# Masked down product over pairs of ring places, with its loads and its search reordered

## The chip, the cores and the metric

One Trainium2 chip, one core. The metric is the device time of one execution in microseconds; lower is better.

## The reference

Four residual sublayers over 2,048 tokens (two sequences of 1,024) of width 512: causal attention with 32 heads of 16, an FFN with 4-bit quantised weights (inner width 1,792), a masked MLP (inner width 1,376), and the same FFN again. The change lies in the masked MLP:

```python
s = silu(x @ w_gate.T)                      # x: layernormed, 1376 wide
_, idx = top_k(-abs(s), 688)                # the 688 smallest of each row
s = s with zeros at idx
y = (s * (x @ w_up.T)) @ w_down.T           # back to 512 wide
```

## The kernel before

`phase_project` and `phase_attend` run first (until about 670 us) and are not touched. `phase_mlp` (L1190) does the FFN, the masked MLP and the second FFN.

**Chunks and stages.** The tokens are eight chunks (`NC = 8`) of 256, each of two tiles of 128 (`TPC = 2`, t = 0, 1). A chunk k goes through four stages: f1 k (FFN), gates k, down k, f2 k (FFN). `mlp_order` (L1822) interleaves the stages of several chunks: f1 0, gates 0, f1 1, f1 2, gates 1, **down 0**, f1 3, gates 2, f2 0, **down 1**, f1 4, gates 3, f2 1, **down 2**, f1 5, gates 4, **down 3**, f2 2, gates 5, f1 6, **down 4**, f2 3, gates 6, f1 7, **down 5**, f2 4, gates 7, **down 6**, f2 5, f2 6, **down 7**, f2 7. So down 0, 3 and 6 follow their own gates stage at once; before the others there is at least one FFN stage in between.

**Slots.** A stage is a row of slots, one unit of TensorE work each: 14 in an FFN stage (`block_of`, L1497, and two slots behind it `product`, L1511), 8 in gates (`gate_unit`, L1521: four column blocks, each for both tiles), 8 in down (`product_tk`, L1539). What every other engine does is written into the slots by `mlp_stages` (L1837), and each engine walks the slots in the same order. Operands are split into fp16 high and low halves, so that each product is three matmuls.

**The masked path.** After gates k, VectorE and ScalarE search each row's threshold in 31 trials (`search`, L1646; `signs`, L1580), then VectorE finishes the masks in 18 items (`finish`, L1662): 7 for tile 0, 11 for tile 1. Behind a tile's last item come `mask` on GpSimd (L1459, two halves), `masked_high` on ScalarE (L1613), `masked_low` on GpSimd (L1465), and the **turn** (`turn_masked`, L1413): one DMA transpose of the tile from ax to pp, issued by SyncE three slots after the first mask. Down k multiplies the turned tiles by w_down.

**Where the search is paced.** L1907 to L1922 spread the items over the slots: `costs` are the items' times, `spans` those of a slot on TensorE (3860 ns in an FFN stage, 3460 in gates, 1950 in down), and the rate is set so that all of a chunk's items are done before the last slots ahead of its down stage, which the end of L1911 leaves out.

**The ring.** Four places (`ring`, L1215) hold either gate and up weights (`load_g`, L1390: eight loads f = 0 to 7 of a gates stage, 688 KB each, place f % 4) or the down weights (`load_d`, L1401: d = 0 to 3, place d; d = 3 is shorter and comes in two DMAs). In down, `product_tk` goes through d = 0 to 3 with tile 0 and then with tile 1, 9, 9, 9 and 6 matmuls each; d = 0 first waits for the tile's turn (`mt_in`), and each d with tile 0 for its place. Places come free as tile 1 is done with them: loads of the next gates stage wait for `DG + f + 1` units. In a gates stage, loads f = 4, 5 stand in slot 1, f = 6, 7 in slot 3 (they wait for 4 units), d = 0, 1 in slot 5 (6 units) and d = 2, 3 in slot 7 (8 units).

**The shifts.** The normed input of a coming stage is transposed by two DMA transposes (`Norm.shift`, L1310), one a tile, from d_xs to xT. In a gates stage both stand in slot 5, for the stage after it (or the one after the down stage, where down comes next).

**SyncE's queue.** SyncE issues all of these in the order of its program: in each slot first the shifts, then the turns, then the loads, then stores and refills (L1429 to L1442). A wait there holds back all that is behind it.

```python
for u, t in slot.shifts:
    norms[u.name].shift(sp, u, t)
for k, t in slot.masked_turns:
    turn_masked(k, t)
for k, f in slot.gate_loads:
    load_g(k, f)
for k, d in slot.down_loads:
    load_d(k, d)
```

Of the kernel before, what the change touches and what calls it, by code (L numbers as in the profile page):

```python
# [1189 lines left out]
def phase_mlp(nc, ident, w_gate, w_up, w_down, wgu_scr, wd_scr, x1_scr, out):  # L1190

    TPC = 2
# [6 lines left out]
    DG = -(-TKB // DB)  # L1199
    DU = TPC * DG  # L1200
    RING = 4
    XR = 5
# [6 lines left out]
    with ExitStack() as ctx:  # L1209
# [173 lines left out]
        def _(sp):  # L1383
# [6 lines left out]
            def load_g(k, f):  # L1390
                c, m, r = f // 2, f % 2, f % RING
                if f >= RING:
                    wait(sp, gm_ok, GU * k + TPC * (c - 1))
                elif k == 1:
                    wait(sp, gm_ok, TPC * ((f + RING) // 2 + 1))
                elif k > 1:
                    wait(sp, dm_ok, DU * (k - 2) + DG + f + 1)
                sp.dma_start(ring[r][:, 0:2 * KB * TKW], wgu_scr[m, c].rearrange("p a k w -> p (a k w)")
                             ).then_inc(ring_in[r], 16)

            def load_d(k, d):  # L1401
                if k + 1 < NC:
                    wait(sp, gm_ok, GU * (k + 1) + TPC * (3 + d // 2))
                else:
                    wait(sp, dm_ok, DU * (k - 1) + DG + d + 1)
                full = min(DB, TKB - 1 - DB * d)
                sp.dma_start(ring[d][:, 0:full * 2 * D].rearrange("p (j w) -> p j w", j=full),
                             wd_scr[DB * d:DB * d + full].rearrange("j p a d -> p j (a d)")).then_inc(ring_in[d], 16)
                if full < DB:
                    sp.dma_start(ring[d][0:ROWS_LAST, full * 2 * D:(full + 1) * 2 * D],  # L1410
                                 wd_scr[TKB - 1, 0:ROWS_LAST].rearrange("p a d -> p (a d)")).then_inc(ring_in[d], 16)
# [17 lines left out]
            for s in stages:  # L1429
                for slot in s.slots:  # L1430
                    for u, t in slot.shifts:
                        norms[u.name].shift(sp, u, t)
                    for k, t in slot.masked_turns:
                        turn_masked(k, t)
                    for k, f in slot.gate_loads:
                        load_g(k, f)
                    for k, d in slot.down_loads:
                        load_d(k, d)
                    for done in slot.stores:
                        store(done)  # L1440
                    for c in slot.refills:
                        load_x(c)  # L1442
# [53 lines left out]
        def _(pe):  # L1496
# [42 lines left out]
            def product_tk(s, v):  # L1539
                k, t, d = s.c, v // DG, v % DG  # L1540
                if d == 0:
# [98 lines left out]
        def _(dve):  # L1640
# [79 lines left out]
            def take_in(s, t):  # L1720

                if s.kind == "down":
                    dve.wait_ge(dm_ok, DU * s.c + DG * (t + 1))
                else:
                    dve.wait_ge(dn_ok, JB * (s.f + 1))
# [94 lines left out]


def mlp_order(NC):  # L1822

# [13 lines left out]
def mlp_stages(NC, GU, DU, TPC, RING, DG, XR):  # L1837
# [70 lines left out]
    for n, (p, slot, span, duty) in enumerate(own):  # L1908
        rate = 0
        for k in range(NC):  # L1910
            ahead = [(l, d) for q, _slot, l, d in own[n:] if q < at["down", k]][:-2]  # L1911
            left = sum(costs[item] for c, item in items if c <= k)
# [10 lines left out]
    assert not items  # L1923

    everywhere = [slot for s in stages for slot in s.slots]
    for n, slot in enumerate(everywhere):
# [9 lines left out]
    for k in range(NC):  # L1936
        for f in range(2 * TKC):
# [4 lines left out]
            elif k > 1:  # L1942
                stages[at["down", k - 2]].slots[DG + f].gate_loads.append((k, f))
        for d in range(DG):
            if k + 1 < NC:
                stages[at["gates", k + 1]].slots[TPC * (3 + d // 2) - 1].down_loads.append((k, d))
            else:
                stages[at["down", k - 1]].slots[DG + d].down_loads.append((k, d))
    for p, s in enumerate(stages[:-1]):
# [35 lines left out]
```

## Time and profile before

| | |
|---|---|
| median of 3 runs | 1968.83 us (1966.81 to 1973.61) |
| the profiled execution | 1973.73 us, its span 1971.9 us |
| TensorE busy, matmul | 1837.5 us, 93% of the span |
| VectorE busy | 1430.5 us, 73% |
| ScalarE busy | 1031.7 us, 52% |
| GpSimd busy | 762.1 us, 39% |
| mean granted TensorE clock | 0.977 of full speed |
| DMA q1 (issued by SyncE) | 187.77 MB, 33.5% of 16 engines' span |

The busy share is of the whole span, phases with other limits included; `ring<-wd_scr` is a load of down weights, `ring<-wgu_scr` one of gate or up weights, `pp<-ax` a turn and `xT_f<-d_xs` a shift. `acc<-ring,pp` is the masked down product, `ga<-ring,xT_g` and `ub<-ring,xT_g` are the two halves of a gate unit.

### The profile page before, as it was taken

How to read it: one execution, taken by the hardware profiler on the slowest of the kernel's cores; microseconds unless marked ns; L12 is line 12 of the kernel's file. 1: busy time of each engine (PE TensorE's matmuls, PEld its weight loads, DVE VectorE, ACT ScalarE, POOL GpSimd, SP SyncE). 2: the span in 40 equal slices, each digit the busy share in tenths (PEclk: the TensorE clock that was granted, in tenths of full speed). 3: DMA queues.
4: the chain of work that ended last, by engine and by line, in shares of the span. 5: the costliest groups of instructions: out<-in, count | busy, mean ns of one | idle time of the engine just before them, and what ended most of it. 6: DMA issues, size and time to landing. Idle time of an engine off the chain costs nothing.

```text
span 1971.9 us, 39587 instructions
## 1 busy us (share of the span) xinstructions
PE 1837.5 (93%) x14968; PEld 1123.6 (57%) x14968; DVE 1430.5 (73%) x2798; ACT 1031.7 (52%) x1888; POOL 762.1 (39%) x922
## 2 busy tenths in 40 slices
PE   7998888898899798999999999999999999989979
PEld 3443333333333475775776776666776766747746
DVE  6567778788882313987888988887888789869821
ACT  4234677777785122654654645535546546536411
POOL 4685756566762111223215124132151151322331
PEclk9998899999999898999999999999999999999989
DMA  7864544555434604106131331225142142071010
GB/s 236 236 198 141 151 118 122 139 149 159 147 112 125 218 1 126 12 12 176 49 126 42 90 125 42 90 75 144 57 122 73 40 133 73 12 201 34 12 40 12
DMA packets 217133, 205.70 MB, mean 104 GB/s; under 512 B 136400, under 2 KB 173264, under 8 KB 216992
## 3 DMA queue, kind: packets, MB, share of 16 engines
q1 hardware_dynamic: 210992, 187.77, 33.5%
q0 software_dynamic: 4272, 12.91, 2.0%
q10 hardware_dynamic: 1728, 3.15, 0.4%
q8 instruction: 87, 1.43, 0.3%
q14 instruction: 54, 0.44, 0.1%
HBM read 147.39 MB, written 33.62 MB: 92 GB/s over the span
## 4 chain that ended last, share of the span: by engine, by line
PE 53%; DVE 5%; POOL 3%; issue 2%; DMA 2%; ACT 1%; SPq 0%; DVEq 0%; ACTq 0%
PE acc L1517 13%; PE ga L1507 13%; PE ub L1507 13%; PE acc L1550 5%; PE ga L1535 5%; PE ub L1535 5%; POOL pp L1463 1%; DVE kept L1701 1%; DMA ring<-wd_scr 1%; DMA ring<-wgu_scr 1%; POOL ax L1469 1%; DVE kept L1698 1%; DVE kept L1696 0%; POOL lohi L1453 0%; POOL rstd_f L1271 0%
## 5 line engine op out<-in xcount | busy, mean ns | idle before, releaser
L1453 POOL TENSOR_TENSOR lohi<-h,lohi 128x256 f16<-128x256 f32 x224 | 177.0, 790 | 732.5 <-ACT lohi L1598 732.3
L1587 ACT ACTIVATE kept<-ax,T 128x1376 f16<-128x1376 f32 x248 | 357.3, 1441 | 138.8 <-DVE T L1659 134.8
L1651 DVE TENSOR_SCALAR_CACHE_REDUCE junk<-ax,T 128x1376 f16<-128x1376 f32 x248 | 406.1, 1638 | 0.9
L1067 ACT ACTIVATE pr<-s 128x512 f32<-128x512 f32 (+2 forms) x640 | 320.6, 554 | 97.7 <-PE s L956 77.2
L649 DVE TENSOR_REDUCE mx<-s 128x2 f32<-128x1024 f32 (+2 forms) x300 | 320.0, 1114 | 67.2 <-PE s L628 35.2
L1507 PE MATMUL ga<-xT_f,w_gate 128*128 128x256 f16 x2688 | 333.4, 274 | 11.8 <-DVE h L1708 7.6
L1507 PE MATMUL ub<-xT_f,w_up 128*128 128x256 f16 x2688 | 333.9, 275 | 0.0
L1517 PE MATMUL acc<-w_down,lohi 128*128 128x512 f16 x1344 | 326.4, 379 | 2.1 <-POOL lohi L1453 2.0
L1507 PEld LDWEIGHTS ga<-xT_f,w_gate 128*128 128x128 f16 x2688 | 263.2, 98 | 88.1 <-DVE h L1708 13.3
L1507 PEld LDWEIGHTS ub<-xT_f,w_up 128*128 128x128 f16 x2688 | 264.9, 99 | 32.3
L1708 DVE SCALAR_TENSOR_TENSOR h<-ub,g 128x256 f32<-128x256 f32 x224 | 94.1, 420 | 183.7 <-ACT g L1593 183.6
L1517 PEld LDWEIGHTS acc<-w_down,lohi 128*128 128x128 f16 x1344 | 131.1, 98 | 118.5 <-POOL lohi L1453 4.1
L1593 ACT ACTIVATE g<-ga 128x256 f32<-128x256 f32 x224 | 84.4, 377 | 192.3 <-PE ub L1507 191.8
L968 PE MATMUL po<-pr,Va 128*32 128x512 f32 (+3 forms) x1536 | 164.1, 508 | 0.2 <-ACT pr L1067 0.2
L950 PE MATMUL s<-Q,K 49*128 49x512 f16 (+3 forms) x768 | 127.1, 340 | 31.8 <-ACT pr L1067 16.9
L1598 ACT ACTIVATE lohi<-h 128x256 f16<-128x256 f32 x224 | 91.5, 408 | 109.2 <-DVE h L1708 75.0
L1535 PE MATMUL ga<-ring,xT_g 128*128 128x344 f16 x768 | 125.5, 314 | 10.3 <-DMA ring<-wgu_scr 8.8
L1550 PE MATMUL acc<-ring,pp 128*128 128x512 f16 (+1 forms) x528 | 122.4, 390 | 13.0 <-DMA ring<-wd_scr 7.6
L950 PEld LDWEIGHTS s<-Q,K 49*128 49x128 f16 x768 | 37.4, 94 | 154.3 <-ACT pr L1067 135.8
L1535 PE MATMUL ub<-ring,xT_g 128*128 128x344 f16 x768 | 123.0, 310 | 0.6 <-DMA ring<-wgu_scr 0.6
L628 PE MATMUL s<-K,Q 48*128 48x512 f16 (+2 forms) x720 | 109.9, 336 | 8.4 <-DVE mx L649 4.4
L1659 DVE TENSOR_SCALAR T<-T,pat,nextb 128x1 int32<-128x1 int32 x496 | 112.7, 269 | 0.0
(179 smaller groups left out, 2659.5 us busy)
## 6 DMA issues: line engine op xcount, KB each, us to landing
ring<-wgu_scr SPq DMA_DIRECT2D x64, 688.0 KB, 5.4
ring<-wd_scr SPq DMA_DIRECT2D x24, 768.0 KB, 6.2
wgu_scr<-tk_h POOLq DMA_DIRECT2D x32, 172.0 KB, 2.7
q_scr<-qk_h SPq DMA_DIRECT2D x16, 256.0 KB, 2.6
k_scr<-qk_h SPq DMA_DIRECT2D x16, 256.0 KB, 4.5
v_scr<-v_f SPq DMA_DIRECT2D x16, 256.0 KB, 5.3
Q<-q_scr SPq DMA_DIRECT2D x64, 64.0 KB, 2.1
K<-k_scr SPq DMA_DIRECT2D x64, 64.0 KB, 2.1
```

What stands on the lines that cost most here:

```text
L649: self.nc.vector.tensor_reduce(dst.rearrange("p (t j) -> p t j", t=NT)[:, :, p0:p1], scores.rearrange("p t (j k) -> p t j k", k=w), AX.X, ...
L950: mm = nc.tensor.matmul(o[t], K[i][rows, p, kb * P:(kb + 1) * P], Q[i][rows, p, f * BANK + lo:(f + 1) * BANK], start=True, stop=not diag)
L968: mm = nc.tensor.matmul(po[32 * j:32 * j + 32, lo:BANK], Va[i][:, kb, j, :], pr[:, g % NPR, j, 0:BANK - lo], start=(kb == 0), stop=(g + 1 ...
L1067: nc.scalar.activation(pr[:, g % NPR, NP * t + p0:NP * t + p1, 0:w], scores, ACT.Exp, scale=SCALE).then_inc(e2_ok, 1)
L1453: nc.gpsimd.tensor_tensor(hT[j % 2][:, 1, :], h[j % 2][:, :], hT[j % 2][:, 0, :], ALU.subtract).then_inc(hl_ok, 1)
L1507: m = nc.tensor.matmul(bank[:, 0:CW], w[:, a, k, j * P:(j + 1) * P], norm.xT[:, b, k, :], start=(n == 0), stop=(n == len(ops) - 1))
L1517: m = nc.tensor.matmul(acc(s, t)[:, :], hT[j % 2][:, a, t * P:(t + 1) * P], w_down[:, b, j, :], start=(j == 0 and a == 0 and b == 0), stop ...
L1535: mm = nc.tensor.matmul((ga, ub)[m][v % 2][:, 0:TKW], norms["g"].xT[:, a, kb, t * P:(t + 1) * P], wr[:, b, kb, :], start=(n == 0), stop=(n ...
L1550: m = nc.tensor.matmul(acc(s, t)[:, :], turned[k % 2][0:w, t, a * TKB + j, :], wr[:, b, :], start=(j == 0 and a == 0 and b == 0), stop=(j ...
L1587: nc.scalar.activation(kept[0][:, :], ax[k % 2][:, 1, 0:I_TK], ACT.Sign, scale=-1.0, bias=TF[:, 1:2], accum_out=cnt[:, 1:2]).then_inc(c1_o ...
L1651: nc.vector.tensor_scalar(junk[:, :], ax[k % 2][:, 0, 0:I_TK], TF[:, 0:1], -float(KZERO), ALU.is_lt, ALU.add, accum_out=cnt[:, 0:1]).then_ ...
L1659: nc.vector.tensor_scalar(T[:, t:t + 1], T[:, t:t + 1], pat[:, t:t + 1], nextb[:, i:i + 1], ALU.bitwise_xor, ALU.bitwise_xor).then_inc(u_o ...
```

## The change

`down_order` puts the units of a down stage in the order (t, d) = (0,0), (0,1), (1,0), (1,1), (0,2), (0,3), (1,2), (1,3). The waits for freed places, the slots of the loads that use them and VectorE's wait for a finished tile follow from it: places 0 to 3 are free after units 3, 4, 7 and 8 (before: 5, 6, 7, 8), and tile 0's sum is complete after unit 6 (before: 4). SyncE issues a slot's ring loads ahead of its shifts and turns. The planner leaves out the last three slots ahead of a chunk's down stage in place of two.

```diff
+def down_order(TPC, DG):
+    return [(t, d) for d0 in range(0, DG, 2) for t in range(TPC) for d in range(d0, min(d0 + 2, DG))]
...
+    order_down = down_order(TPC, DG)
+    freed = [order_down.index((TPC - 1, d)) for d in range(DG)]
+    ended = [order_down.index((t, DG - 1)) for t in range(TPC)]
...
-                    wait(sp, dm_ok, DU * (k - 2) + DG + f + 1)
+                    wait(sp, dm_ok, DU * (k - 2) + freed[f] + 1)
...
-                    wait(sp, dm_ok, DU * (k - 1) + DG + d + 1)
+                    wait(sp, dm_ok, DU * (k - 1) + freed[d] + 1)
...
+                    for k, f in slot.gate_loads:
+                        load_g(k, f)
+                    for k, d in slot.down_loads:
+                        load_d(k, d)
                     for u, t in slot.shifts:
                         norms[u.name].shift(sp, u, t)
                     for k, t in slot.masked_turns:
                         turn_masked(k, t)
-                    for k, f in slot.gate_loads:
-                        load_g(k, f)
-                    for k, d in slot.down_loads:
-                        load_d(k, d)
...
-                k, t, d = s.c, v // DG, v % DG
+                k, (t, d) = s.c, order_down[v]
...
-                    dve.wait_ge(dm_ok, DU * s.c + DG * (t + 1))
+                    dve.wait_ge(dm_ok, DU * s.c + ended[t] + 1)
...
-            ahead = [(l, d) for q, _slot, l, d in own[n:] if q < at["down", k]][:-2]
+            ahead = [(l, d) for q, _slot, l, d in own[n:] if q < at["down", k]][:-3]
...
-                stages[at["down", k - 2]].slots[DG + f].gate_loads.append((k, f))
+                stages[at["down", k - 2]].slots[freed[f]].gate_loads.append((k, f))
...
-                stages[at["down", k - 1]].slots[DG + d].down_loads.append((k, d))
+                stages[at["down", k - 1]].slots[freed[d]].down_loads.append((k, d))
```

## Rows read from the trace of the kernel before

**Rows 1.** Waits of TensorE, 740 to 1972 us: line, releaser, total us, times, longest

```profile
PE ga L1535 <- DMA ring<-wgu_scr: 8.8, 3, 3.4
...
PE ga L1507 <- DVE h L1708: 7.6, 9, 2.6
PE acc L1550 <- DMA ring<-wd_scr: 7.6, 4, 2.8
```

**Rows 2.** TensorE in order of time, down 7: start, us, work, count [idle before <- releaser]

```profile
1884.66 3.50 PE L1550 MATMUL acc<-ring,pp 128*128 128x512 f16 x9 [4.80 <-issue]
...
1892.52 10.53 PE L1550 MATMUL acc<-ring,pp 128*128 128x512 f16 x48
```

**Rows 3.** TensorE in order of time, end of gates 1, down 0, start of f1 3

```profile
912.82 1.91 PE L1535 MATMUL ga<-ring,xT_g 128*128 128x344 f16 x12 [2.10 <-DMA ring<-wgu_scr]
...
921.85 7.56 PE L1550 MATMUL acc<-ring,pp 128*128 128x512 f16 x33 [1.87 <-DMA ring<-wd_scr]
...
937.09 1.48 PE L1507 MATMUL ga<-xT_f,w_gate 128*128 128x256 f16 x12
```

**Rows 4.** TensorE in order of time, units 6 and on of gates 4, down 3, start of f2 2

```profile
1329.26 1.91 PE L1535 MATMUL ga<-ring,xT_g 128*128 128x344 f16 x12 [3.44 <-DMA ring<-wgu_scr]
1331.72 1.92 PE L1535 MATMUL ub<-ring,xT_g 128*128 128x344 f16 x12 [0.55 <-DMA ring<-wgu_scr]
...
1336.98 4.05 PE L1550 MATMUL acc<-ring,pp 128*128 128x512 f16 x18
1343.62 12.22 PE L1550 MATMUL acc<-ring,pp 128*128 128x512 f16 x48 [2.59 <-DMA ring<-wd_scr]
1355.68 1.47 PE L1507 MATMUL ga<-xT_f,w_gate 128*128 128x256 f16 x12
```

**Rows 5.** TensorE in order of time, gates 7, down 6, start of f2 5

```profile
1744.85 3.23 PE L1535 MATMUL ga<-ring,xT_g 128*128 128x344 f16 x12 [3.29 <-DMA ring<-wgu_scr]
...
1760.49 12.23 PE L1550 MATMUL acc<-ring,pp 128*128 128x512 f16 x48 [2.82 <-DMA ring<-wd_scr]
1772.55 1.48 PE L1507 MATMUL ga<-xT_f,w_gate 128*128 128x256 f16 x12
```

**Rows 6.** Busy times of engines in down 3; after them granted clock, DMA share, GB/s

```profile
1336.90:1355.80 18.90, 16.31 (x70) 6.92 (x69) 17.12 (x45) 11.71 (x16) 2.08 (x2) 0.91 0.72 190
```

**Rows 7.** SyncE in order of time, gates 4 to down 3, and the last turns

```profile
1321.30 2.76 SPq L1416 DMA_TRANSPOSE pp<-ax  x1
1324.11 1.04 SPq L1398 DMA_DIRECT2D ring<-wgu_scr  x2
1325.55 6.04 SPq L1317 DMA_TRANSPOSE xT_f<-d_xs  x2
...
1339.06 6.01 SPq L1416 DMA_TRANSPOSE pp<-ax  x1
...
1880.16 11.07 SPq L1416 DMA_TRANSPOSE pp<-ax  x2
```

**Rows 8.** DMA issues by line, whole span: last number is median us to landing

```profile
xT_f<-d_xs SPq DMA_TRANSPOSE x28, 2.7
...
pp<-ax SPq DMA_TRANSPOSE x16, 4.4
```

**Rows 9.** DMA issues of 1017.2 to 1019 us (loads d), and of 1339 to 1340 us

```profile
ring<-wd_scr SPq DMA_DIRECT2D x2, 768.0 KB, 5.6
...
pp<-ax SPq DMA_TRANSPOSE x1, 8.0
```

**Rows 10.** All engines in order of time, slots 6 and 7 of gates 2, start of f2 0

```profile
1014.22 2.59 SPq L1317 DMA_TRANSPOSE xT_f<-d_xs  x2
...
1019.90 1.36 PE L1507 MATMUL ga<-xT_f,w_gate 128*128 128x256 f16 x11
```

**Rows 11.** The shifts' line, 1322 to 1338 us: ns of issue, first and last start; landing

```profile
L1317 SPq DMA_TRANSPOSE xT_f<-d_xs x2: 1578/2574/3571, 1325.5 to 1328.0; - x2
...
DMA to landing us min/median/max: 5.6/6.4/7.2
```

More of the change, by code:

```diff
@@ L1923, in mlp_stages @@
     assert not items
+    freed = [down_order(TPC, DG).index((TPC - 1, d)) for d in range(DG)]
     everywhere = [slot for s in stages for slot in s.slots]
```

## The prediction

> **What bounds the kernel now.** I read the waits of TensorE first, over the MLP phase [rows 1]. TensorE sets the pace there, and little is left to win: its waits on ring transfers are 8.8 + 7.6 us and on VectorE's h 7.6 us; one of 4.80 us, whose releaser the profile doesn't name, stands ahead of the last chunk's first masked down product [rows 2]. The change can only move these, or add to them.
>
> TensorE's order of time then shows where the ring waits sit [rows 3, 4, 5]. Only three down stages (chunks 0, 3, 6) follow their gates stage at once; the other four before the tail have an FFN stage between, and their weights and turns are early. In gates 4, unit 6 starts 3.44 us late; after gates 4 ends at 1336.98, two ring places are used up in 4.05 us and TensorE idles 2.59 us for the third. The 48 matmuls behind that take 12.22 us against 10.53 in the last chunk [rows 2, 4]; the granted clock of down 3 averages 0.91 of full speed, so some of it ran at the 1.2 GHz level [rows 6]. Gates 7/down 6 repeat it: 3.29 us, 3.23 us for twelve matmuls that take 1.91, then 2.82 us [rows 4, 5]. Gates 1/down 0 show 2.10 and 1.87 us [rows 3].
>
> SyncE's order gives the cause [rows 7]. The turn of tile 0 goes out at 1321.30, and the loads of ring places 2 and 3 only at 1324.11, though unit 3 freed them at about 1318.8: unit 6 could have begun at 1329.26 - 3.44 = 1325.82, and a unit is 3.50 us (1331.72 to 1336.98 is three half units [rows 4]). Places 0 and 1 are loaded behind two shifts, whose issue ends at 1331.6.
>
> **The change, part by part.** The lead of three first. The planner's arithmetic, with `[:-3]` for `[:-2]`, moves tile 0's turn of chunks 3 and 6 from slot 2 of the gates stage to slot 1, and of chunk 7 from slot 11 of f2 6 to slot 10. Chunk 0's stays in slot 2. Tile 1's turn goes from slot 0 of down 0, 3, 6 and 7 to the last slot of the stage before.
>
> *Gates 4 and 7.* With the turn a slot ahead, places 2 and 3 are asked for when unit 3 ends. The first lands 5 to 6 us later (now 1329.26 - 1324.11 = 5.15) and unit 6 wants it 7.0 us later. Gain: 3.44 + 0.55 (a second short wait for the other place) = 4.0 us in gates 4; 3.29 + (3.23 - 1.91) = 4.6 us in gates 7. Gates 1 keeps its 2.10 us: there the turn is still in slot 2, ahead of slot 3's loads, and the reorder works only inside one slot. Sum -8.6.
>
> *Down 0, 3, 6.* The new order is two places with tile 0, the same two with tile 1, then the other two. The wait for place 2 goes, since 36 matmuls now cover it. What is late next is tile 1's turn. Down needs it after 18 matmuls, 3.9 us after the gates stage ends, where it needed it after 33. But SyncE issues it after loads d = 2, 3, which wait for all 8 gate units, that is for the stage's end. Issue: three loads at about half a us each, so 1.6 us after the end at the earliest. Landing: 4.4 us alone [rows 8], which gives 6.0 as the low bound; in down 3 it took 8.0 us from 1339.06 [rows 7, 9], 10.1 after the end, the high bound. I take 9.0: the loads ahead of it still go out at the stage's end, and only the earlier backlog is lighter. So TensorE idles 9.0 - 3.9 = 5.1 us, and then has 48 matmuls at the slow start's 12.2. Down lasts 21.2 us, against 17.1 (919.98 to 937.09), 18.7 and 18.9 (1772.55 less 1753.62, which is 1760.49 - 2.82 - 4.05) now [rows 3, 4, 5]: +4.1 +2.5 +2.3 = +8.9.
>
> *Tail.* The 4.80 us before down 7 is the turn of tile 0, a slot (3.9 us by the planner's constant 3860) too late. One slot earlier leaves about 1 us, and the slow start goes too: 3.50 us for nine matmuls now, of which 10.53 / 48 x 9 = 2.0 is needed [rows 2]. That is -3.8 - 1.5 = -5.3. Tile 1's turn, also a slot earlier, lands near 1888.9: SyncE's two turns end at 1880.16 + 11.07 = 1891.2, so the second, 2.8 us long like the others, went out at 1888.4; 3.9 less is 1884.5, and 4.4 to land [rows 7, 8]. It is wanted after two units and two leftover products, as now the 48 matmuls begin 1892.52 - 1884.66 = 7.9 after the start, 1.5 of it slow: 6.4 after 1880.9, at 1887.3. That is 1.6 us of wait. Sum -3.7, bounds -5.3 to 0 (0 if VectorE can't finish the search earlier).
>
> *Loads ahead of shifts.* In gates 2, 3, 5 and 6 the two shifts of slot 5 make xT for the very next stage. In gates 2 they go out from 1014.22 on and, alone, need 2.7 us [rows 8, 10]: in time for 1019.90. Now the loads d = 0, 1 go first, as soon as six units are done (T = 1019.90 - 7.0 = 1012.9). The second lands at T + 0.55 + 5.6 = T + 6.15 [rows 9]. What happens to shifts behind loads stands in gates 4: the loads issued at 1324.11 landed by 1331.6 (unit 6's second half began 1331.72), the shifts issued at 1325.55 and 1328.0 after 7.2 and 5.6 us, so at 1332.8 and 1333.6 [rows 4, 7, 11]: 1.9 us behind the load. T + 8.05 against a need at T + 7.0 gives 1.0 us. Gates 0 has two smaller loads in their place, about the same. Five stages: +5.0, bounds 0 (shifts pass loads) to +12.8 (each with a slow start like gates 7's 1.3 us, and half a us of issue).
>
> Here a rule of the Trainium skill speaks against this part. The Trainium skill, DMA: Bandwidth & Descriptors, section "Queues, rings and completion order", says that each DMA engine takes descriptors in ring order, and that completion need not keep that order. By ring order a shift waits for the loads, and the +5.0 stands; were its second half to decide, the +5.0 would fall to 0. Gates 4's rows agree with ring order.
>
> *At nothing:* the earlier release of places 0 and 1 (an FFN stage lies before their next use), and tile 0's take-in in slot 6, which now waits for six units; VectorE is busy with search trials until then, and no TensorE step hangs on it for 5 us. If that cover went, the cost is TensorE's h wait of [rows 1].
>
> **Sum.** -8.6 + 8.9 - 3.7 + 5.0 = +1.6 us on the profiled execution's 1973.7. That execution is 4.9 above the median of the three runs, 1968.8, so the forecast of the median is 1970. Within 0.3% (5.9 us), which is about what a measurement of this kernel can tell from no change.
>
> **Rivals.** *Turns come in time (faster).* If the DMA engines mix transposes with loads, tile 1 lands at the 6.0 bound, saving 3.0 us three times, and the shifts cost nothing, -5.0: -14 in all, so 1956; if only the slow starts go (three times 1.7), 1965. For it: the DMA backlog of gates 4 is partly the lateness itself. Against: gates 4's shifts. Chance 0.27 that it is past 0.3%.
>
> *Stage starts (slower).* The shifts land later than 1.0 us past the need in the five stages. Place: the first FFN matmul after gates 0, 2, 3, 5, 6. Price: up to 12.8 in place of 5.0, so 1978. It decides once a late shift costs over 1.9 us a stage. For it: a shift's own issue took 3.57 us behind loads [rows 11]. Against: gates 1's 2.10 us wait left its matmuls at 1.91 us, unslowed [rows 3]. Chance 0.15.
>
> *The lead isn't gained.* POOL, not the search, may hold tile 0's turn: its low halves stand behind rstd in the same slot. Then the 8.6 us stay and the time is 1978. Against it: in the new plan chunk 3's last low half is in slot 1, ahead of the rstd. Chance 0.10.
>
> **Numbers.** Forecast 0.48, faster 0.27, slower 0.15 + 0.10 = 0.25. The range 1958 to 1980 reaches the two slower cases and most of the faster one. Within it the forecast's own range is 1964 to 1976.
>
> **What would show it.** Right: no wait for wgu_scr in gates 4 and 7, about 2 us still in gates 1; in down 0, 3 and 6 one wait after 18 matmuls with DMA pp<-ax as releaser, 4 to 6 us, and none for wd_scr; about 1 us at the first matmul of f1 1, f2 0, f2 1, f2 3 and f1 7 with xT_f<-d_xs as releaser; down 7 starting near 1881. Wrong: waits on pp<-ax under 2.5 us, or on xT_f over 1.9 us a stage, or a grown total of waits on h.

## The result, and the profile after

The changed kernel takes 1985.23 us (median of 4 runs, 1983.49 to 1987.60) against 1969.32 for the kernel before (4 runs of the same session): ratio 1.0079, 95% interval 1.0057 to 1.0101. It is slower by 0.8%, 15 us above the forecast, outside its range and above the 1978 of both slower rivals.

The profiled execution is near the lower end of the four, 1983.73 us with a span of 1981.9, against 1973.73 and 1971.9 for the kernel before. The first matmul of f1 0, where TensorE's MLP work begins and which the change does not reach, starts at 679.70 in it and at 683.87 in the profile before. From there to the end are 1302.2 us against 1288.0: **+14.2 us in the MLP phase**, close to what the medians show (+15.9). The start of that work moves by some 14 us from execution to execution (673 to 687 us in the profiles below, with no order by kernel), so I compare kernels by the length from it to the end, called the MLP length from here on, and by stage lengths (from the first matmul of a stage to the first of the next). Medians stand beside them. Every MLP length is that of one profiled execution, and so is the 1288.0 that all are set against.

TensorE's waits of the kernel after, 740 to 1985 us (line, releaser, total us, times, longest):

```profile
PE acc L1553 <- DMA pp<-ax: 21.1, 4, 7.4
PE ga L1510 <- DMA xT_f<-d_xs: 13.5, 5, 3.0
...
PE acc L1520 <- POOL lohi L1456: 5.2, 2, 2.6
PE ga L1538 <- DMA ring<-wgu_scr: 4.9, 1, 4.9
...
PE acc L1553 <- issue: 1.2, 1, 1.2
PE ga L1510 <- DVE h L1711: 0.5, 1, 0.5
```

Against [rows 1]: the waits for down weights (7.6 us) are gone, those on h fell from 7.6 to 0.5 and on gate weights from 8.8 to 4.9. Two that did not exist are 34.6 us together: the turns, and the shifts.

TensorE in order of time, same kernel; the lines are f1 1's start, unit 6 of gates 1 and down 0, f2 0's start, down 3, f1 6's start, the end of down 6, and down 7:

```profile
776.08 1.48 PE L1510 MATMUL ga<-xT_f,w_gate 128*128 128x256 f16 x12 [2.23 <-DMA xT_f<-d_xs]
...
911.81 3.25 PE L1538 MATMUL ga<-ring,xT_g 128*128 128x344 f16 x12 [4.94 <-DMA ring<-wgu_scr]
...
920.14 4.05 PE L1553 MATMUL acc<-ring,pp 128*128 128x512 f16 x18
929.11 13.44 PE L1553 MATMUL acc<-ring,pp 128*128 128x512 f16 x48 [4.91 <-DMA pp<-ax]
...
1028.04 1.49 PE L1510 MATMUL ga<-xT_f,w_gate 128*128 128x256 f16 x12 [2.67 <-DMA xT_f<-d_xs]
...
1338.03 4.05 PE L1553 MATMUL acc<-ring,pp 128*128 128x512 f16 x18
1348.65 11.90 PE L1553 MATMUL acc<-ring,pp 128*128 128x512 f16 x48 [6.57 <-DMA pp<-ax]
...
1771.52 12.09 PE L1553 MATMUL acc<-ring,pp 128*128 128x512 f16 x48 [7.36 <-DMA pp<-ax]
...
1891.83 2.10 PE L1553 MATMUL acc<-ring,pp 128*128 128x512 f16 x9 [1.19 <-issue]
...
1900.73 12.21 PE L1553 MATMUL acc<-ring,pp 128*128 128x512 f16 x48 [2.27 <-DMA pp<-ax]
```

The lines answer to [rows 2 to 5]. Down 0, 3 and 6 now stop after 18 matmuls for tile 1's turn, and the 48 behind take 11.9 to 13.4 us where 10.53 is full speed [rows 2]. The busy times of down 3 with its granted clock (third number from the end) show it at 22.4 us and a clock of 0.85, against 18.9 and 0.91 [rows 6]:

```profile
1338.00:1360.40 22.40, 15.83 (x69) 6.72 (x67) 17.22 (x45) 11.69 (x16) 2.00 (x2) 0.85 0.71 179
```

SyncE in order of time, same kernel, gates 1 to down 0, gates 2, gates 4 to down 3:

```profile
904.05 2.84 SPq L1419 DMA_TRANSPOSE pp<-ax  x1
...
921.80 5.19 SPq L1419 DMA_TRANSPOSE pp<-ax  x1
...
1018.39 0.90 SPq L1410 DMA_DIRECT2D ring<-wd_scr  x2
1019.51 6.47 SPq L1320 DMA_TRANSPOSE xT_f<-d_xs  x2
...
1324.22 0.95 SPq L1401 DMA_DIRECT2D ring<-wgu_scr  x2
...
1340.56 5.96 SPq L1419 DMA_TRANSPOSE pp<-ax  x1
```

In gates 4 the loads at 1324.22 now find their places without delay, so that part does what it should. But each turn of tile 1 (921.80, 1340.56) goes out only when the gates stage has ended (920.14, 1338.03) and the loads d = 2, 3 are issued, and each pair of shifts stands behind two loads (688 KB each in gates 0, 768 KB each in the others). In gates 4 the second shift's issue itself ends only at 1338.8, 0.8 us behind the end of the stage, and the loads and the turn behind it are late by that much more. The loads d = 0, 1 of gates 2 and the two shifts behind them, from their lines' views (ns of one issue, first and last start; us to landing):

```profile
L1410 SPq DMA_DIRECT2D ring<-wd_scr x2: 370/430/489, 1018.4 to 1018.8; - x2
...
DMA to landing us min/median/max: 4.7/6.0/7.3
```

```profile
L1320 SPq DMA_TRANSPOSE xT_f<-d_xs x2: 2305/3214/4123, 1019.5 to 1021.9; - x2
...
DMA to landing us min/median/max: 6.1/6.9/7.6
```

The shifts landed 7.6 and 6.1 us after issue, at 1027.1 and 1028.0, the second of them 1.9 us behind the second load (1026.1); the median shift of the kernel before takes 2.7 [rows 8], and in gates 2 its two went out at 1014.22 in 2.59 us [rows 10].

Lengths of TensorE's stages in us. "Shifted" is gates 0, 2, 3, 5, 6 together, behind which TensorE can wait for a shift (it is counted to the stage before it); "tail" is f2 5, f2 6 and down 7:

| kernel | shifted | gates 1 + down 0 | gates 4 + down 3 | gates 7 + down 6 | tail | rest | MLP length |
|---|---|---|---|---|---|---|---|
| before | 152.6 | 50.1 | 53.6 | 54.8 | 137.1 | 839.8 | 1288.0 |
| after | 166.2 | 59.3 | 53.0 | 54.1 | 136.1 | 833.6 | 1302.2 |
| order_alone | 166.5 | 49.3 | 51.7 | 52.6 | 139.1 | 837.8 | 1297.1 |
| lead_alone | 152.7 | 56.2 | 55.1 | 51.7 | 132.7 | 837.6 | 1285.9 |
| pairs_alone | 152.5 | 55.7 | 57.1 | 58.1 | 139.3 | 837.6 | 1300.2 |
| after_old_order | 151.9 | 52.7 | 49.8 | 48.4 | 134.5 | 837.5 | 1274.8 |
| one_load_ahead | 155.4 | 49.7 | 51.8 | 52.1 | 138.1 | 838.1 | 1285.2 |
| turns_first | 166.7 | 51.6 | 49.8 | 49.1 | 136.1 | 838.5 | 1291.9 |
| lead_not_chunk0 | 166.9 | 54.6 | 53.3 | 54.5 | 134.6 | 837.9 | 1301.8 |
| gate_loads_first | 152.8 | 52.8 | 50.3 | 49.2 | 136.2 | 839.2 | 1280.4 |
| down_loads_where_free | 152.5 | 52.4 | 49.5 | 49.2 | 136.9 | 840.3 | 1280.8 |
| lead4 | 156.7 | 48.8 | 51.5 | 48.3 | 132.5 | 839.6 | 1277.3 |
| lead5 | 153.9 | 53.1 | 47.8 | 53.7 | 132.7 | 842.7 | 1284.0 |
| lead5_loads_free | 153.6 | 46.4 | 46.2 | 46.5 | 132.1 | 844.5 | 1269.4 |
| best_again | 153.7 | 46.7 | 46.1 | 46.4 | 132.2 | 844.6 | 1269.7 |
| best_without_pairs | 153.0 | 52.1 | 51.8 | 49.3 | 132.1 | 841.3 | 1279.5 |

lead5_loads_free and best_again are one kernel; their rows show how closely stage lengths repeat. Of lead4's 11 runs one took 2175.87 us at a granted clock of 0.824, against 0.976 to 0.985 in the others, and is left out of its ratio.

### The profile page after: what moved, and what is told of

It reads as the page before. It is cut to its first block, busy times and chain, and to the rows that moved or that the text cites. A ratio compares the mean times of both kernels' runs of the same rounds, so it can differ in the third digit from the quotient of the medians.

```text
span 1981.9 us, 39587 instructions
## 1 busy us (share of the span) xinstructions
PE 1835.4 (93%) x14968; PEld 1123.8 (57%) x14968; DVE 1426.8 (72%) x2798; ACT 1031.0 (52%) x1888; POOL 754.0 (38%) x922
## 4 chain that ended last, share of the span: by engine, by line
PE 52%; POOL 5%; DMA 3%; DVE 3%; issue 2%; SPq 1%; ACT 1%; DVEq 0%; ACTq 0%
PE acc L1520 13%; PE ga L1510 13%; PE ub L1510 13%; PE acc L1553 5%; PE ga L1538 4%; PE ub L1538 4%; DMA xT_f<-d_xs 2%; POOL d_xs L1311 1%; DMA pp<-ax 1%; POOL lohi L1456 1%; SPq L1320 1%; POOL ax L1472 1%; POOL rstd_f L1274 1%; POOL pp L1466 1%; DVE junk L1654 1%
## 5 line engine op out<-in xcount | busy, mean ns | idle before, releaser
L1456 POOL TENSOR_TENSOR lohi<-h,lohi 128x256 f16<-128x256 f32 x224 | 171.6, 766 | 750.7 <-ACT lohi L1601 750.3
L1590 ACT ACTIVATE kept<-ax,T 128x1376 f16<-128x1376 f32 x248 | 356.9, 1439 | 154.6 <-DVE T L1662 150.9
```

Source lines behind the costliest of these rows:

```text
L1456: nc.gpsimd.tensor_tensor(hT[j % 2][:, 1, :], h[j % 2][:, :], hT[j % 2][:, 0, :], ALU.subtract).then_inc(hl_ok, 1)
L1590: nc.scalar.activation(kept[0][:, :], ax[k % 2][:, 1, 0:I_TK], ACT.Sign, scale=-1.0, bias=TF[:, 1:2], accum_out=cnt[:, 1:2]).then_inc(c1_o ...
```

## The experiments

### The three parts, one at a time

**order_alone**: the kernel before with only SyncE's new order.

```diff
                 for slot in s.slots:
+                    for k, f in slot.gate_loads:
+                        load_g(k, f)
+                    for k, d in slot.down_loads:
+                        load_d(k, d)
                     for u, t in slot.shifts:
```

> The kernel before, with only SyncE's order changed: in each slot the ring loads go out ahead of the shifts and turns. Theory A (the shifts behind two ring loads are the largest part of the loss): TensorE waits 2 to 3 us for xT_f<-d_xs at the start of f1 1, f2 0, f2 1, f2 3 and f1 7, 13 us in all, and gates 1, 4, 7 and the down stages stay within 2 us each of before; the median is 11 to 15 us above before. Rival B (the order costs only what the prediction had, 1.0 us a stage, and the rest of the change's loss comes from the new down order): +3 to +6 us.

Measured: 1973.14 us (10 runs), ratio 1.0034 (1.0016 to 1.0052); MLP length +9.0. Its waits, 740 us to the end:

```profile
PE ga L1507 <- DMA xT_f<-d_xs: 13.0, 5, 2.9
```

The five shifted stages carry +13.9, by the waits as expected; the time was not, +6.8 us by the medians where 11 to 15 was expected. The three pairs of stages with a turn are 4.9 us shorter, not longer: tile 1's turn has 33 matmuls of cover in the old down order. The expectation names f2 3, as the prediction does, but the stage behind gates 5 is f1 6, and there the wait is.

**lead_alone**: the kernel before with the lead of three.

```diff
-            ahead = [(l, d) for q, _slot, l, d in own[n:] if q < at["down", k]][:-2]
+            ahead = [(l, d) for q, _slot, l, d in own[n:] if q < at["down", k]][:-3]
```

> The kernel before, with only the planner's lead changed ([:-3]). Theory A (the lead is a gain on its own): the 4.0 and 4.6 us waits for wgu_scr in gates 4 and gates 7 go, the wait of 4.8 us ahead of down 7 shrinks to about 1, the FFN stages' waits on h shrink by some 5 us, and gates 1 gets some 4 us longer, because the scan of tile 1 now runs beside GpSimd's rstd: 10 to 15 us below before. Rival B (the lead only pays together with the new order of loads): within 3 us of before.

Measured: 1967.26 us (10 runs), ratio 1.0019 (0.9996 to 1.0043); MLP length -2.1. Its waits and, in order of time, down 3:

```profile
PE acc L1550 <- DMA ring<-wd_scr: 14.2, 5, 4.0
...
PE ga L1535 <- DMA ring<-wgu_scr: 4.8, 1, 4.8
...
PE ga L1507 <- DVE h L1708: 3.2, 6, 1.2
```

```profile
1332.54 5.73 PE L1550 MATMUL acc<-ring,pp 128*128 128x512 f16 x18 [2.43 <-DMA ring<-wd_scr]
1342.28 12.22 PE L1550 MATMUL acc<-ring,pp 128*128 128x512 f16 x48 [4.01 <-DMA ring<-wd_scr]
```

Rival B was right. The 4.0 us on gate weights and 4.4 us on h that the lead wins come back as 6.6 us more on down weights [rows 1]. At the third place it is 4.0 us more: the earlier turn of tile 1 stands ahead of the loads d = 2, 3, which the old down order needs after 18 matmuls. At the first place, where down 3 and 6 now wait 2.4 and 2.3 us, it is 2.9 us more.

**pairs_alone**: `down_order` and the waits that follow from it; the old SyncE order and the lead of two.

```diff
-                k, t, d = s.c, v // DG, v % DG
+                k, (t, d) = s.c, order_down[v]
...
-                wait(sp, dm_ok, DU * (k - 2) + DG + f + 1)
+                wait(sp, dm_ok, DU * (k - 2) + freed[f] + 1)
```

> The kernel before, with only the new order of the down units (pairs of ring places for both tiles) and the places' waits and slots that follow. Theory A (the wait for place 2 is traded for an earlier need of tile 1's turn): down 0, 3 and 6 wait 4 to 7 us for pp<-ax after 18 matmuls and each is 3 to 6 us longer than before, the rest is as before; +10 to +14 us. Rival B (pairs hide the load of place 2 and tile 1's turn lands in time): the 1.9, 2.6 and 2.8 us waits for wd_scr go and the total is 5 to 8 us below before.

Measured: 1979.83 us (8 runs), ratio 1.0078 (1.0054 to 1.0103); MLP length +12.1. Its waits:

```profile
PE acc L1553 <- DMA pp<-ax: 15.4, 3, 6.0
```

The waits for down weights go (0.9 us are left), and twice as much comes back for tile 1's turn. With a lead of two that turn stands in slot 0 of the down stage.

**after_old_order**: the changed kernel with the old SyncE order (shifts, turns, gate loads, down loads).

```diff
-                    for k, f in slot.gate_loads:
-                        load_g(k, f)
-                    for k, d in slot.down_loads:
-                        load_d(k, d)
...
                         turn_masked(k, t)
+                    for k, f in slot.gate_loads:
+                        load_g(k, f)
+                    for k, d in slot.down_loads:
+                        load_d(k, d)
```

> The changed kernel with SyncE's old order (shifts and turns ahead of the slot's loads). Theory A: the five waits on xT_f<-d_xs go (13.5 us), and tile 1's turn, now ahead of loads d = 2, 3, lands 1 to 3 us earlier in down 0, 3 and 6; 15 to 21 us below the changed kernel, so 1964 to 1970. Rival B (loads d = 2, 3 behind a turn that waits for GpSimd come too late, and TensorE then waits for wd_scr instead): only the 13 us of the shifts are won, or less, and waits for wd_scr of over 2 us a stage stand in down 0, 3 and 6: 1972 or more.

Measured: 1960.65 us (10 runs), ratio 0.9968 (0.9942 to 0.9994); MLP length -13.2. Its waits:

```profile
PE ga L1538 <- DMA ring<-wgu_scr: 5.3, 1, 5.3
PE acc L1553 <- DMA ring<-wd_scr: 4.7, 2, 2.4
PE acc L1553 <- DMA pp<-ax: 3.5, 3, 2.4
```

The gain is past theory A's 1964; of rival B's waits on down weights 4.7 us came, at the first place of down 3 and 6. So pairs and lead together give -13.2, though alone they give +12.1 and -2.1: each repairs what the other spoils. The lead puts tile 1's turn ahead of the loads d = 2, 3; the pairs let TensorE need that turn first and those loads only after 36 matmuls. The new order undoes exactly this and costs 27.4 us on top of the two, against 9.0 on the kernel before. In the medians the gain is 5.7 us with an interval of 1.2 to 11.4 (0.0006 and 0.0058 of 1966): the stage lengths of the one profile say more than the runs confirm, and only the sign and the places are sure.

### What the new order costs, and why

**one_load_ahead**: order_alone with the load d = 1 behind the shifts again, so that one load of 768 KB stands ahead of them.

```diff
                     for k, d in slot.down_loads:
-                        load_d(k, d)
+                        if d != 1:
+                            load_d(k, d)
                     for u, t in slot.shifts:
                         norms[u.name].shift(sp, u, t)
+                    for k, d in slot.down_loads:
+                        if d == 1:
+                            load_d(k, d)
```

> The kernel before with loads ahead of shifts and turns, but in slot 5 of a gates stage load d = 0 goes out ahead of the shifts and load d = 1 behind them. Theory A (the shifts wait for the data of the loads ahead of them, in ring order): with one load of 768 KB less ahead, some 2.0 us of flow, the waits for xT_f<-d_xs at f2 0, f2 1, f2 3 and f1 7 fall from 2.6 to 2.9 us each to 0 to 1 us; f1 1, which has gate loads ahead, keeps its 2.3. Rival B (a plain load in flight costs a transposing DMA a fixed time, whatever its size): they stay over 2 us.

Measured: 1966.09 us (8 runs), ratio 0.9992 (0.9972 to 1.0011); MLP length -2.8. Its wait on shifts:

```profile
PE ga L1511 <- DMA xT_f<-d_xs: 2.1, 1, 2.1
```

The one left is at f1 1, whose gates stage has gate loads and keeps both of them ahead. With one load less ahead the other four waits, 2.6 to 2.9 us in order_alone, are gone; the load's issue is half a us of that. A shift waits for the data that is in the queue ahead of it: in gates 2 of this kernel the one load lands at 1015.4 and the second shift 1.9 us behind it, the same distance as behind two loads in the changed kernel.

**turns_first**: the changed kernel with the turns ahead of the loads, the shifts still behind them.

```diff
+                    for k, t in slot.masked_turns:
+                        turn_masked(k, t)
                     for k, f in slot.gate_loads:
...
                         norms[u.name].shift(sp, u, t)
-                    for k, t in slot.masked_turns:
-                        turn_masked(k, t)
```

> The changed kernel, but in a slot the turns go out ahead of the ring loads; the loads stay ahead of the shifts. Theory A (the loss has two parts of like size: the shifts behind loads, and tile 1's turn behind loads d = 2, 3): the five waits for xT_f<-d_xs stay at 13 to 14 us, and gates 1, 4, 7 with down 0, 3, 6 together get 10 to 15 us shorter than in the changed kernel (166 us), close to the 151 us they take with the whole old order. Rival B (loads d = 0, 1 ahead of the shifts are what fills the queues): they stay above 160 us.

Measured: 1970.54 us (8 runs), ratio 1.0014 (0.9992 to 1.0037); MLP length +3.8. Its waits:

```profile
PE ga L1510 <- DMA xT_f<-d_xs: 13.1, 5, 3.0
...
PE acc L1553 <- DMA pp<-ax: 7.5, 3, 2.9
```

This splits the 27.4 us: the three gates and down pairs drop from 166.4 to 150.5, as in after_old_order (150.9), while the shifted stages stay at 166.7. The drop is in down 0, 3 and 6 (68.1 to 51.6 us), while gates 1 keeps its 37 us. Some 16 us are tile 1's turn behind loads, some 14 us are the shifts behind loads, 1.6 are in the tail; the stages in "rest" give 4 back.

### Gates 1

After the change gates 1 waits 4.94 us, where it waited 2.10 [rows 3]. The turn of tile 0 went out 2.8 us ahead of the end of unit 5 (904.05 against 911.81 - 4.94 = 906.87) and 5.4 us ahead before (905.27 against 910.72). Ahead of it GpSimd had this to do, beside this on VectorE (all engines in order of time, kernel after):

```profile
899.02 3.02 DVE L1699 TENSOR_TENSOR_SCAN kept<-junk 128x1376 f16<-128x1376 f16 x1
899.19 3.33 POOL L1274 TENSOR_TENSOR rstd_f<-rstd_f,d_neghalf 128x2 f32<-128x2 f32 x1 [8.33 <-DVE rstd_f L1288]
```

**lead_not_chunk0**: the changed kernel with a lead of two for chunk 0 alone, which moves that scan.

```diff
-            ... if q < at["down", k]][:-3]
+            ... if q < at["down", k]][:-3 if k else -2]
```

> The changed kernel with the planner's old lead (two slots) for chunk 0 and three for the others. Theory A (the longer gates 1 comes from GpSimd's rstd running beside VectorE's scan of tile 1, which the new plan puts into slot 2): the rstd of gates 1 takes 0.7 us again in place of 3.33, the turn of tile 0 goes out 2 us or more earlier against unit 3, and the wait for wgu_scr in gates 1 falls from 4.94 to about 2.2 us. Rival B (the wait comes from the ring loads' own order or from the DMA queue): it stays over 4 us.

Measured: 1982.32 us (4 runs), ratio 1.0090 (1.0058 to 1.0122); MLP length +13.8, gates 1 33.0 in place of 37.0. GpSimd in order of time:

```profile
895.43 0.69 POOL L1274 TENSOR_TENSOR rstd_f<-rstd_f,d_neghalf 128x2 f32<-128x2 f32 x1 [6.77 <-DVE rstd_f L1288]
```

With the scan only at 900.57 the same instruction takes 0.69 us, 2.64 less, and the wait is 2.2 us again. Gates 1 with down 0 is 4.7 us shorter (down 0 21.7 us for 22.2), but the MLP length only 0.4: the stages in "rest" are 4.3 us longer in this profile, f2 0 alone 2.9, at a granted clock of 0.94 for 1.00. So it is one collision, worth about 2.7 us of wait and, with the slower matmuls behind it, 4 us of gates 1, and it would not have saved the forecast.

**gate_loads_first**: old order but gate loads ahead of turns, and loads f = 4 to 7 one slot earlier. **down_loads_where_free**: the same, and loads d = 0, 1 ahead of the shifts in the three gates stages whose next stage is down.

```diff
-                stages[at["gates", k]].slots[TPC * (f // 2 - 1) - 1].gate_loads.append((k, f))
+                stages[at["gates", k]].slots[TPC * (f // 2 - 1) - 2].gate_loads.append((k, f))
```

```diff
+                    early = after is not None and s.kind == "gates" and after.kind == "down" and n == TPC * 3 - 1
+                    if early:
+                        for k, d in slot.down_loads:
+                            load_d(k, d)
                     for u, t in slot.shifts:
```

> The changed kernel with SyncE's order in a slot: shifts, gate loads, turns, down loads; and with the gate loads of places a stage refills itself (f = 4 to 7) one slot earlier, so that f = 6, 7 go out before chunk 0's turn of tile 0. Theory A (what costs is a ring load queued behind a turn that is not ready, and a shift queued behind ring loads; each is cured apart): against the changed kernel with SyncE's old order, the 5.35 us wait for wgu_scr in gates 1 and its slow start go, gates 1 is 5 to 8 us shorter, all else stays; some 10 us under the kernel before by the median of many runs, 18 to 21 us in the MLP phase. Rival B (in gates 1 the turn then lands later and the wait moves to down 0): gates 1 and down 0 together gain less than 3 us.

> As the kernel with gate loads first, but where a down stage comes next (gates 1, 4, 7), loads d = 0, 1 go out ahead of slot 5's shifts, which nothing needs for another 14 us. Theory A: the 2.4 and 2.3 us waits for wd_scr at the start of down 3 and down 6 go, and tile 1's turn is no later: 3 to 6 us below the kernel with gate loads first, in the MLP phase. Rival B (the DMA queues are full there, so what is loaded earlier makes tile 1's turn later by as much): down 3 and 6 wait for pp<-ax instead and the sum stays within 1.5 us.

Measured: 1964.71 us (12 runs), ratio 0.9990 (0.9973 to 1.0007), MLP length -7.6; and 1959.95 us (12 runs), ratio 0.9968 (0.9949 to 0.9986), MLP length -7.2. The first one's waits:

```profile
PE acc L1553 <- DMA ring<-wd_scr: 9.9, 3, 4.9
...
PE acc L1553 <- DMA pp<-ax: 3.4, 2, 2.4
```

and the second one's:

```profile
PE acc L1558 <- DMA pp<-ax: 12.2, 4, 4.9
```

Rival B was right both times. The wait for gate weights in gates 1 goes in both, and gates 1 with down 0 stays at 52.8 and 52.4 us against 52.7. In the first, loads d are late by 4.93 us; once those are early, the turn is, by 4.91. While tile 0's turn is issued in the middle of the stage, putting one transfer ahead only makes another late.

### A longer lead, and the best version

**lead4** and **lead5**: after_old_order with a lead of four and of five. **lead5_loads_free**: down_loads_where_free with a lead of five; **best_again** is the same kernel in more rounds.

```diff
-            ... if q < at["down", k]][:-3]
+            ... if q < at["down", k]][:-5]
```

> The changed kernel with SyncE's old order and a lead of four slots in place of three. Theory A (tile 1's turn is what the paired order waits for, so a slot more of lead takes its waits away, and tile 0's turn leaves the slot of the rstd in gates 1): waits for pp<-ax under 1 us in all, no wait for wgu_scr; gates 1, 4, 7 with down 0, 3, 6 take 140 to 146 us against 151 with a lead of three, the waits on h and lohi grow by less than 4 us; 5 to 10 us below the lead of three. Rival B (VectorE has no slack left for a faster search): the waits on h and lohi grow by as much as is won.

> As the lead of four, with five slots. Theory A: nothing is left to win in the down stages (within 2 us of the lead of four there), and waits on h and lohi grow: the MLP phase is within 3 us of the lead of four, more likely above. Rival B: still 3 us or more to win, from the shifts and loads that then stand clear of the turns.

> Lead of five with the order: shifts, gate loads (a slot earlier), turns, down loads, and loads d = 0, 1 ahead of the shifts where a down stage is next. Theory A (with the turns early, DMA has room and the 2.3 us waits for wd_scr at the start of down 3 and 6 go): gates 1, 4, 7 with down 0, 3, 6 take 134 to 139 us (44.9 us a pair without a wait). Rival B (full queues): over 141 us.

> The same kernel as lead5_loads_free, run again in more rounds: pairs of places, a lead of five slots, shifts ahead of loads, gate loads a slot earlier, the down loads ahead of the shifts where a down stage follows. Theory: its MLP phase is 18.7 us shorter than before's (1269.4 against 1288.0), so its median is 14 to 20 us below the kernel before. Rival: its two timed runs were lucky in the phases ahead of the MLP, and the median is only 5 to 10 us below. The stage lengths of its trace repeat within 1 us, and its waits on xT_f are none, on wd_scr 2 us, on pp<-ax under 2 us.

Measured: lead4 1958.04 us (11 runs), ratio 0.9960 (0.9939 to 0.9981), MLP length -10.8; lead5 1964.47 us (12 runs), 0.9981 (0.9962 to 0.9999), -4.0; lead5_loads_free 1948.13 us (2 runs), 0.9904 (0.9870 to 0.9939), -18.7; best_again 1949.39 us (6 runs), 0.9923 (0.9901 to 0.9945), -18.3. That a longer lead gives more by itself was a miss: lead4 ends 2.5 us above lead 3 in MLP length, lead5 9.2. For lead4 the medians don't bear this out (it is 2.6 us below lead 3), so the two can't be told apart; in its profile the three pairs are 2.3 us shorter, and the shifted stages 4.8 us longer, where TensorE waits for VectorE (2.21 us at f2 1, 1.45 at f1 7). In lead5 gate weights are waited for again, and the first place of down 0, that for 5.41 us ahead of the stage's first matmul:

```profile
PE acc L1553 <- DMA ring<-wd_scr: 7.5, 4, 5.4
PE ga L1538 <- DMA ring<-wgu_scr: 5.8, 3, 3.2
```

With each load at its first free moment, the lead pays. Waits of best_again:

```profile
PE ga L1515 <- DVE h L1716: 10.0, 8, 2.1
PE acc L1525 <- POOL lohi L1461: 4.7, 4, 1.8
...
PE acc L1558 <- DMA ring<-wd_scr: 1.9, 3, 0.8
PE acc L1558 <- DMA pp<-ax: 1.6, 1, 1.6
```

TensorE in order of time, down 0 of the same kernel, and SyncE at the end of gates 1:

```profile
905.75 4.05 PE L1558 MATMUL acc<-ring,pp 128*128 128x512 f16 x18
911.45 10.53 PE L1558 MATMUL acc<-ring,pp 128*128 128x512 f16 x48 [1.65 <-DMA pp<-ax]
```

```profile
906.73 3.05 SPq L1419 DMA_TRANSPOSE pp<-ax  x1
909.82 1.11 SPq L1410 DMA_DIRECT2D ring<-wd_scr  x2
```

There tile 1's turn goes out 1.0 us after the gates stage's end (906.73 against 905.75; 1.7 in the changed kernel), but ahead of the loads d = 2, 3, and lands 5.7 us after that end (911.45) in place of 9.0; 1.65 us of wait leave the 48 matmuls at 10.53. The three pairs of stages take 46.7, 46.1 and 46.4 us. Without a wait a gates stage takes 30.59 us (gates 1 here) and a down stage right behind one 14.25 (down 0 of after_old_order), 44.8 in all, so 1.3 to 1.9 us are left there. What grew is the wait for h, 7.6 to 10.0 us: the search now lies in FFN slots, and the two FFN stages f2 0 and f1 6 are 1.8 and 3.1 us longer.

**best_without_pairs**: best_again with the down order of before.

```diff
-    return [(t, d) for d0 in range(0, DG, 2) for t in range(TPC) for d in range(d0, min(d0 + 2, DG))]
+    return [(t, d) for t in range(TPC) for d in range(DG)]
```

> best_again with the down order of before (four places with tile 0, then four with tile 1) and nothing else changed. Theory: pairs of places give time once nothing holds up the turns and the loads, so without them the first use of places 2 and 3 comes at once and the loads of d = 2, 3, which wait for the end of the gates stage, are late: waits on wd_scr of 2 to 3 us in each of down 0, 3 and 6, and the MLP phase 6 to 10 us longer than best_again's. Rival: the pairs contribute nothing, all of the gain is the lead of five and the loads' places; then the MLP phase is within 2 us of best_again's.

Measured: 1962.22 us (12 runs), ratio 0.9982 (0.9962 to 1.0003); MLP length -8.5, 9.8 above best_again. Its waits, and TensorE in down 0:

```profile
PE acc L1558 <- DMA ring<-wd_scr: 13.1, 6, 4.8
```

```profile
912.51 4.05 PE L1558 MATMUL acc<-ring,pp 128*128 128x512 f16 x18
921.36 12.82 PE L1558 MATMUL acc<-ring,pp 128*128 128x512 f16 x48 [4.80 <-DMA ring<-wd_scr]
```

Much as the theory had it: one wait at the third place of 4.80, 3.45 and 2.67 us in down 0, 3 and 6, where 2 to 3 was expected, two of them with a slow start. The paired down product is worth half of the best version's gain in MLP length (12.8 of 16.9 us by the medians), though by itself it cost 12.1 us.

## Why the prediction was wrong

Predicted +1.6 us, measured +14.2 in the MLP phase. Step by step:

- **Gates 4 and 7** (-8.6): right. Neither waits for gate weights; they are 4.3 us and 5.2 us shorter, 9.6 in all.
- **Gates 1** (0): wrong. The step said "Gates 1 keeps its 2.10 us". The slot stayed, but within it GpSimd's rstd grew by 2.64 us beside a scan; the wait is 4.94 us and the twelve matmuls behind it take 3.25 in place of 1.91. +4.0. The third rival had GpSimd as what holds tile 0's turn, and its rstd by name, but for gates 4 and 7 and as a matter of queue order.
- **Down 0, 3, 6** (+8.9): the mechanism was right, tile 1's turn behind loads d = 2, 3 and a stop after 18 matmuls; the size was low. TensorE has it 9.0, 10.6 and 11.6 us after the gates stage's end, where I took 9.0, and the waits are 4.91, 6.57 and 7.36 us for 5.1. The argument for staying under the high bound of 10.1, "only the earlier backlog is lighter", did not hold: from 1340.56 to 1348.65 the turn took 8.1 us, as before [rows 9]. Nor did the issue 1.6 us after the stage's end: it held in down 0 (921.80), but in down 3 and 6 SyncE was still issuing shifts when the stage ended, and the turn went out after 2.5 and 3.6 us (1340.56, 1763.55). The three stages take 22.2, 22.4 and 23.5 us against 21.2. Measured against [rows 3 to 5] by stage length, with the wait of 1.87 us ahead of the old down 0 counted to it as in the prediction: +5.1, +3.7 and +4.6, so +13.4 for +8.9.
- **Loads ahead of shifts** (+5.0, bounds 0 to +12.8): this is the step that failed most. The mechanism was right and one term mis-sized, the landing of the second load. It was put at T + 0.55 + 5.6, the shifts 1.9 us behind it, so at T + 8.05 against a need at T + 7.0. They came 2.2 to 3.0 us late in each of the five stages, +13.6 in all. f2 0 wanted the shifts of gates 2 at 1028.04 - 2.67 = 1025.37, so T (7.0 before) is 1018.37, and the loads were issued at T itself, at 1018.39. The second load went out at 1018.81 and landed 7.3 us later, at T + 7.7; the second shift landed 1.9 us behind it, as forecast, but at T + 9.6. In all five stages the second load takes 6.9 to 7.6 us and the second shift lands 1.9 to 2.0 us behind it. The 5.6 was the median of two loads of which the second, with no shifts behind it, took 6.2 [rows 9]; and gates 4, from where the 1.9 came, has its second load go out at 1324.7 and land by 1331.7, which is 6.9 us. With both terms from gates 4 the sum is T + 0.55 + 6.9 + 1.9 = T + 9.4, 2.4 us a stage and +12 in all. The rival's condition, over 1.9 us a late stage, was met in all five. Its price of 12.8 was nearly the measured 13.6 by luck, being made of other parts: the 13.6 is wait. The first twelve matmuls behind it take 1.48 us at f1 1 and 1.49 at f2 0; slow matmuls follow only at f1 6 (1.87 us, the next twelve 2.77) and f1 7 (1.50, then 2.74), and they are in the column "rest". The stage behind gates 5 is f1 6, not the f2 3 that the prediction names.
- **Tail** (-3.7): -1.0. The 4.80 us wait is 1.19, as forecast, but the turn of tile 1 is 2.27 us late for 1.6, and the 48 matmuls behind it take 12.21 for 10.53, a slow start that I had counted as gone.
- **FFN waits** (0): the total on h fell from 7.6 to 0.5 us while that on GpSimd's low halves rose from 2.0 to 5.2; f2 1 is 5.5 us shorter and f1 7 1.8, f1 6 2.2 us longer: -6.3 in the column "rest". Not forecast; it hid a third of the loss.

Sum of the misses: shifts 8.6, gates 1 4.0, the down stages 4.5, tail 2.7, gates 4 and 7 -1.0, rest -6.3: 12.5, against 14.2 - 1.6 = 12.6.

By ring order, the rule of the Trainium skill, DMA: Bandwidth & Descriptors, section "Queues, rings and completion order", a shift starts behind the loads ahead of it, and one_load_ahead agrees: four waits of some 2.8 us go with one load of 768 KB less. The rule speaks for the direction; how far behind was for the rows to tell, and I took two parts of one sum from two rows, one of them a median.

The chance went wrong in one more way. I priced the parts as a sum, and they act on each other: alone or without the third they give +9.0, -2.1, +12.1 and -13.2. What the new order costs depends on which transfer the down order needs first. That the gain was lost to the order and not to the pairs or the lead is shown by after_old_order, turns_first and best_again.

What stays open: why the medians of after_old_order, gate_loads_first and best_without_pairs lie 7.5, 6.4 and 4.5 us closer to the kernel before than their MLP lengths do, where the others agree within some 3 us. The phases ahead of the MLP vary by more than that. All but order_alone, turns_first and lead5_loads_free stand higher by their medians than by their MLP lengths, by 1.2 us or more, so the one profile of the kernel before may have an MLP length that is a us or two above its usual one.

## What to carry to other kernels

A queue that is issued in program order has to be sorted by need, and by need again whenever the consumer's order changes: here a transpose wanted after 18 matmuls was put behind loads wanted after 36, and two parts that were worth 13 us together by MLP length (some 6 by the medians) became a loss of 14. When a change has parts that touch the same queue, price them in pairs and not only one by one; and where a small transfer is put behind a large one, take the landing of the large one and the distance behind it from the same row, one in which the small one really stood behind it.

## What the runs showed of the hardware

- The issue of a DMA transpose on SyncE is held up behind large loads: 2.3 and 4.1 us for one shift behind two loads of 768 KB, where two shifts took 2.59 us together with none ahead [rows 10]. The delay is in the engine's own time, so all behind it is late as well: ahead of down 3 a shift's issue ended at 1338.8, and the loads that could have gone at 1338.03 went out at 1338.87.
- A shift behind plain loads on the same queue lands at nearly the same distance behind the last of them: 1.9 to 2.0 us in all five stages of the changed kernel, behind two loads, and 1.9 to 2.0 us in one_load_ahead, behind one load of 768 KB (gates 2, 3, 5 and 6). The second of two loads with shifts behind it takes 6.9 to 7.6 us to land.
- A GpSimd instruction over 128x2 elements (the rstd of gates 1) took 3.33 us in place of 0.69. It had started 0.17 us after a VectorE scan of 3.02 us and ended 0.48 us after it; 0.69 came back when the scan moved. It agrees with the Trainium skill, SBUF — State Buffer, section "Who interferes with whom", by which VectorE and GpSimd share a pair of ports under an exclusive lock: the scan takes both of its inputs from SBUF.
- A wait is not always followed by slow matmuls: 1.65 us of wait in best_again's down 0 left the 48 at 10.53 us and 2.67 us in f2 0 left twelve at 1.49, while 2.27 us in down 7 was followed by 48 in 12.21.
